# Attention behind a mixture of experts on one core: combines ahead of the normalising, two rooms for the first nine scores, two fills beside the last routed tiles

## The reference, cut to what matters

```
xn = _layernorm(x, axis=-1)
x = x + attn(xn) + ffn(xn)
...
scores = einsum('bshd,bthd->bhst', q, k) / sqrt(16)   # masked above the diagonal
out = softmax(scores) @ v ; out @ Wo + bo
...
routed = sum over a token's six experts of weight * (silu(g) * u) @ w_down
```

## Time and profile before

| what | us |
|---|---|
| median of 3 runs | 731.99 |
| lowest and highest | 728.43, 732.77 |
| the profiled execution: its time | 725.61 |
| its span, first to last instruction | 723.8 |
| PE busy in the span | 674.7 |
| DVE busy | 497.2 |
| POOL busy | 396.6 |
| ACT busy | 326.6 |

### The profile page before, as it was taken

One profiled execution on the slowest core, in us unless ns is written; L12 is line 12 of the kernel. 1 busy time (PEld: TensorE's weight loads), 2 busy tenths in 40 slices (PEclk: granted clock), 3 DMA queues, 4 the chain that ended last, 5 costly groups with the idle time before them and its releaser, 6 DMA issues.

```text
span 723.8 us, 19510 instructions
## 1 busy us (share of the span) xinstructions
PE 674.7 (93%) x5200; PEld 434.2 (60%) x5202; DVE 497.2 (69%) x1184; ACT 326.6 (45%) x849; POOL 396.6 (55%) x383
## 2 busy tenths in 40 slices
PE   6899999989999999999999999999778998999996
PEld 3755677664555555555555555555456776677764
DVE  5498899856666666667666666656377779777751
ACT  2432322224444444444444444444446566656552
POOL 2000000227787777777787776763776776677520
PEclk9599999999999999999999999999989999999998
DMA  8500000037676766767676763342122312231310
GB/s 282 185 1 1 1 0 1 22 112 233 191 211 195 224 211 214 224 211 214 211 224 191 248 210 98 98 96 58 59 66 73 100 55 67 88 98 57 96 59 30
DMA packets 54288, 90.75 MB, mean 125 GB/s; under 512 B 8694, under 2 KB 32438, under 8 KB 54246
## 3 DMA queue, kind: packets, MB, share of 16 engines
q1 hardware_dynamic: 23494, 43.11, 19.9%
q0 software_dynamic: 10752, 29.37, 14.4%
q10 hardware_dynamic: 20000, 17.73, 7.3%
HBM read 69.21 MB, written 20.97 MB: 125 GB/s over the span
## 4 chain that ended last, share of the span: by engine, by line
PE 61%; DVE 9%; POOL 8%; DMA 7%; issue 6%; ACT 3%; DVEq 2%; SPq 2%; ACTq 1%; POOLq 0%
PE pair L1023 20%; PE pair L1058 10%; PE pair L933 6%; POOL wqkv_sb L436 5%; DMA lower<-wdn 5%; PE pair L1009 4%; PE bank L1032 3%; PE pair L1042 3%; PE bank L996 3%; DMA wqkv_sb<-y_rows,slot_i 3%; PE bank L1134 2%; DVE negm L829 2%; DVE space L806 2%; POOL space L432 2%; PE bank L1081 1%
## 5 line engine op out<-in xcount | busy, mean ns | idle before, releaser
L380 POOL DMA_INDIRECT lower<-xn_rows,idx_all x128 | 136.9, 1069 | 228.4 <-DVE idx_all L752 135.5
L1023 PE MATMUL pair<-space,work 128*64 (+1 forms) x768 | 166.0, 463 | 7.9 <-DMA lower<-wdn 3.3
L1058 PE MATMUL pair<-lower,work 88*64 x512 | 121.6, 379 | 1.3 <-ACT work L537 1.0
L1023 PEld LDWEIGHTS pair<-space,work 128*64 128x64 f32 x768 | 66.9, 136 | 80.3 <-issue 56.5
L522 ACT ACTIVATE work<-pair 128x176 f32<-128x176 f32 x160 | 51.5, 322 | 117.4 <-PE pair L1023 59.9
L1058 PEld LDWEIGHTS pair<-lower,work 88*64 88x64 f32 x512 | 69.6, 137 | 48.1 <-issue 11.2
L762 DVE TENSOR_TENSOR work<-work,pair 128x176 f32<-128x176 f32 x160 | 53.1, 333 | 60.5 <-ACT work L522 60.0
L812 DVE COPY space<-lower 88x512 f32 x64 | 78.8, 1231 | 22.2 <-issue 21.8
L1023 PE MATMUL pair<-wqkv_sb,work 128*64 128x352 f32 x256 | 89.4, 472 | 0.0
L529 ACT ACTIVATE lower<-pair 128x256 f32<-128x256 f32 x128 | 49.3, 385 | 77.7 <-PE pair L1058 77.7
L557 ACT ACTIVATE pT<-pair 128x768 f32<-128x768 f32 x64 | 52.0, 812 | 58.9 <-PE pair L1121 56.2
(11 more groups left out here) (171 smaller groups left out, 1346.9 us busy)
## 6 DMA issues: line engine op xcount, KB each, us to landing
space<-wgu SPq DMA_DIRECT2D x66, 352.0 KB
y_rows<-lower ACTq DMA_DIRECT2D x128, 128.0 KB
lower<-wdn SPq DMA_DIRECT2D x66, 176.0 KB
x_all<-x SPq DMA_DIRECT2D x4, 512.0 KB, 7.7
xn_rows<-qk_all SPq DMA_DIRECT2D x16, 128.0 KB, 2.0
lower<-xn_rows,idx_all POOLq DMA_INDIRECT x128
out<-x_all SPq DMA_DIRECT2D x8, 256.0 KB, 2.5
wqkv_sb<-wqkv SPq DMA_DIRECT2D x1, 768.0 KB, 12.5
```

The source lines that it names most:

```text
L380: po.indirect_dma_start(xg[:, r % XB, :], None, xn_rows[:, :], bass.IndirectOffsetOnAxis(idx_all[:, r:r + 1], 0)).then_inc(xg_in[r % XB], 16)
L1023: last = pe.matmul(pair[u % 2][strip, 0:2 * F], xgT[u][:, c, strip], n, start=c == 0, stop=c == EC - 1, skip_group_check=True)
L1058: last = pe.matmul(pair[u % 2][strip, 512:512 + E], hT[:, u % 2, c, strip], n, start=c == 0, stop=c == 1, skip_group_check=True)
```

## The change

Four edits. In `d_slot` the combines of a slot stand directly behind its maxes, ahead of `normalise`, `halves` and `residual`. The scores of m < 9 go to `pair[m % 2]`, and their masks wait for all maxes up to m-2; `turned_masks(0)`, the first other user of `pair[1]`, waits for eight maxes. `fill(0)` and `fill(1)` are issued inside `down` of the last two routed tiles, ahead of its wait for the hidden rows, with waits of their own. The wait for `roped` moves with them.

```
+        def scores_at(m):
+
+            return pair[m % 2 if m < AHEAD else 0][:]
...
             def d_slot(n):
                 if 0 <= n + AHEAD < NS:
                     maxes(n + AHEAD)
+                if 0 <= n + SOONER < NS:
+                    for i in range((n + SOONER) * TOPK * NT // NS, (n + SOONER + 1) * TOPK * NT // NS):
+                        combine(i)
                 if n % 2 == 0 and 0 <= n // 2 - 2 < QUADS:
                     normalise(n // 2 - 2)
                 if n % 8 == 6 and 0 <= (n + 2) // 8 < B:
                     halves((n + 2) // 8)
                 if n % 8 == 5 and 0 <= (n - 13) // 8 < B:
                     residual((n - 13) // 8)
-                if 0 <= n + SOONER < NS:
-                    for i in range((n + SOONER) * TOPK * NT // NS, (n + SOONER + 1) * TOPK * NT // NS):
-                        combine(i)
...
+            def fill(f):
+
+                b, x = f // PAIRS_OF_HEADS, f % PAIRS_OF_HEADS
+                if x == 0:
+                    pe.wait_ge(padded, SB * (b + 1))
+                if f >= 2:
+                    pe.wait_ge(ring_ok, f - 1)
+                else:
+                    pe.wait_ge(xgT_ok, RT)
+                if f == 0:
+                    pe.wait_ge(roped, ROPES * NT)
...
             def down(i, u):
                 e = expert_of(u)
+                if isinstance(i, int) and TILES - 2 <= i:
+                    fill(i - TILES + 2)
                 pe.wait_ge(hT_ok, i + 1)
...
             def score_masks(m):
                 if m:
-                    pe.wait_ge(max_ok, m)
+                    pe.wait_ge(max_ok, m if m >= AHEAD else m - 1)
...
             def turned_masks(n):
                 if n:
                     pe.wait_ge(exp_done, n)
+                else:
+                    pe.wait_ge(max_ok, AHEAD - 1)
...
-                if 0 <= n + FILL < NS:
+                if 2 <= n + FILL < NS:
                     fill(n + FILL)
...
             pe.wait_ge(y_ok, RT)
-            pe.wait_ge(roped, ROPES * NT)
             pe.wait_ge(pad_ok, 1)
```

More of the change, by code:

```diff
@@ L823, in maxes @@
             def maxes(m):
-                scores = pair[0][:].rearrange("p (j k) -> p j k", j=2)
+                scores = scores_at(m).rearrange("p (j k) -> p j k", j=2)
                 dve.wait_ge(s_ok, m + 1)
@@ L1044, in down_shared @@
                 last.then_inc(dn_ok, 1)
+            def fill(f):
[8 more added lines that the diff above has]
+                    pe.wait_ge(roped, ROPES * NT)
+                for a in range(2):
+                    for s in range(SB):
+                        last = pe.transpose(bank[f % 2][:, (a * SB + s) * P:(a * SB + s + 1) * P],
+                                            qkp[:, b % 2, s, a, 2 * x:2 * x + 2].rearrange("p h i d -> p (h i d)"), id_f[:])
+                last.then_inc(tq_ok, 1)
             def down(i, u):
                 e = expert_of(u)
+                if isinstance(i, int) and TILES - 2 <= i:
+                    fill(i - TILES + 2)
                 pe.wait_ge(hT_ok, i + 1)
@@ L1070, in _ @@
             own = [slice(64 * j, 64 * (j + 1)) for j in range(2)]
[L1072 to L1083, removed]
             def score_masks(m):
                 if m:
-                    pe.wait_ge(max_ok, m)
+                    pe.wait_ge(max_ok, m if m >= AHEAD else m - 1)
                 for j in range(2):
-                    o = pair[0][:, 512 * j:512 * (j + 1)].rearrange("p (s k) -> p s k", s=2)[:, :, 0:P]
+                    o = scores_at(m)[:, 512 * j:512 * (j + 1)].rearrange("p (s k) -> p s k", s=2)[:, :, 0:P]
                     pe.matmul(o, id_b[:], mask_b[:].unsqueeze(1).to_broadcast([P, 2, P]), start=True, stop=False,
@@ L1097, in scores @@
                     for j in range(2):
-                        last = pe.matmul(pair[0][:, 512 * j + qt * P:512 * j + (2 * qt + 1) * P],
+                        last = pe.matmul(scores_at(m)[:, 512 * j + qt * P:512 * j + (2 * qt + 1) * P],
                                          q[own[j], qt * P:(qt + 1) * P], k[own[j], 0:(qt + 1) * P],
```

## The result

| | median us | lowest to highest | runs |
|---|---|---|---|
| before, same chip | 732.34 | 728.43 to 734.20 | 6 |
| after | 740.89 | 737.37 to 743.86 | 6 |

The ratio is 1.0125, with a 95% interval of 1.0079 to 1.0170: 9.2 us slower, between 5.8 and 12.4. The profiled execution after took 743.04 us with a span of 741.2, and the mean granted clock is 0.956 where it was 0.981.

The account below looks back on a forecast made before the run. Bound taken: PE at 61% of the span, and in the attention a ring of 24.14 us a batch. 0.4 + 0.05 + 4.15 + 2.2 = 6.8 us on the median 731.99 gave 738.8; range 735.5 to 741.5 (0.60).

Parts of the forecast that it names:

- the ring: Attention: chain from ACT's split through POOL's gathers to DVE's waiting slot 4 combine and the next split; 24.14 us a batch.
- the start: Up to slot 0: fills +0.5, two rooms -0.9, longer low clock +0.8; +0.4 us, bounds -0.9 and +1.8.
- C+0.98: Slot 5: earliest start of PE's projection, 0.98 us after the start C of the waiting slot 4 combine.
- The size of a batch without a fall: Slot 7's maxes and ACT's split 0.83 us later in each of five batches with a projection; 4.15, bounds 2 to 6.2.
- The 0.40 "won back": Slot 6: its combine, 0.40 us, is done during DVE's wait of 0.68 for `back`.
- The clock: PE idle 1.9 to 2.2 us ahead of projections: two of five fall, 1.1 each, 2.2 us; bounds 0 and 8.
- The first batch: Slot 4 without a projection: 0.45 us lost, 0.40 won back in slot 6, 0.05 in sum.
- The fills: Last two `down`s: `fill(0)` free, `fill(1)` delays the last `down`; 0.5 us, between 0 and 0.7.
- rival (b): Clock falls in nearly every batch and in slot 0: 12.5 us slower, 744.5; chance 0.15.
- Rival (d): Start not bound by the gather, two rooms' saving reaches slot 0, batches no longer: 728.5; chance 0.05.
- (c): Projection does not hold PE up, gathers landing earlier or `normalise` finding its place; only the start left: 731.8; chance 0.12.
- Rival (e): Combines delay POOL's subtraction in each batch, 0.48 x 5 on top of the forecast: 741.2; chance 0.08.

Follow-up runs that it names:

- the order alone: Kernel before with the combines of every slot moved ahead of normalise, halves and residual, nothing else; 742.26 us, +9.2 against before.
- slot 4 as before: Changed kernel with normalise ahead of the combines again in the slots 4 modulo 8 only; 727.42 us, -6.2 against before.
- work in the wait: Changed kernel with seven unread matmuls on PE ahead of the projection's wait for normalise; 736.67 us, +5.0 against before.
- the second profile of before: Kernel before, no edit, profiled once more on another chip; 732.17 us (one run).
- the rooms alone: Kernel before with only the first nine scores put in two rooms, fills and combines unmoved; 729.82 us, -2.5 against before.

## Why the prediction was right, and where it was off

The forecast was 738.8, and the median 740.89; on the run's own base, +6.8 against +9.2. The mechanism that carried it is shown: the ring, the projection in slot 5 behind a `normalise` behind the gather, and the falls of the clock. That the number came so near is in part luck: the order costs more than I had, and the start, which I had as a loss, is a gain.

**The projection behind the gather.** C+0.98 was forecast, and it is 0.98, 0.98, 0.99, 0.99 and 0.98. Undoing this one slot removes it.

**The size of a batch without a fall** was mis-sized: 0.83 forecast, 1.35 measured (25.36 against 24.01 for the same batch of before), 1.0 by the order alone (25.31 against 24.29). The forecast's distances of 24.9 to 26 were seen in one batch of the changed kernel; three were 27.0. (My mean of 24.14 runs from the second wait to the sixth, not the fifth; its value stands.) Three pieces make up the 0.52: the batch that I worked out was an unlucky one. Its two casts L841 took 0.42 and in others 0.24, so slot 7's maxes were at C+6.04 in it and at C+5.85 in the batch of 644.75; that is 0.19. The projection held PE 0.10 longer than I had (1.83 us from its start to that of the masks, 658.13 to 659.96, against 1.73); from there to `back` slot 6 took what it took before. And slot 0 took 0.19 more from its maxes to ACT's split (5.06 from 664.12 to 669.18, against 4.87). The 0.40 "won back" by the combine in slot 6 is largely given back there. With slot 4 as before, only that gain should be left, and the ring was 24.02 against 24.01 to 24.07:

```profile
654.41 1.03 DVE negm L833 x2
...
656.58 0.39 PE pair L1131 x4
...
659.48 0.52 ACT space L586
```

Slot 7's maxes start 5.64 after the combine in place of 5.85, but L1131, the products with the transposed maxima, takes 0.39 of the chain where it was 0.25, and the split comes 10.71 after the combine as it did before. That the missing piece is ACT's copy of those maxima, behind its split of slot 6, is argued from the order and not shown.

**The clock.** I counted two falls of 1.1; there were four, and a fall costs 1.6 (27.0 against 25.4; with the order alone there were three). PE's waits were 1.99, 1.93, 1.96, 1.87 and 1.93 us, at or just under the lower end of the 1.9 to 2.2 forecast. This term was 2.2 and measured 6.4 in this execution; with work in the wait it is gone. My way of judging it, by where 2.2 lies between a wait of 1.53 without a fall and one of 2.64 with one, had little under it. With the order alone 2.03 and 1.91 did not fall and 1.88, 1.97 and 1.94 did. And the fall of the earlier trace rows began at 525.5, 0.7 us into the wait of 2.64 (PE's last matmul ahead of it ended at 524.76), while the second profile of before fell at 516.6 behind waits of 1.22 and 0.61.

**The first batch**: 0.05 forecast. With work in the wait the distance behind it was 24.69, in the changed kernel 24.52, against 24.10 before; with the order alone it was 26.09 against 25.63. So 0.4 to 0.6; that this too is what was not won back in slot 6 is argued.

**The start** had the wrong sign: +0.4 forecast, -3.3 (-5.1 to -1.5) measured by itself. "The wait grows by what was saved, and this part brings nothing" held: the wait was 6.29 with the rooms alone, and combine 0 stood 16.9 us behind POOL's split in every profile. In the changed kernel the wait was 3.18 and not the 5 or more that I had announced; the clock was at 0.50 from 516.2 to 523.2 in it, and the early maxes came up to 2.20 apart. The step that failed is the base against which the start was reckoned. I took the low stretch of before to be the 7 us of the first profile, and charged +0.8 for the change making it longer. A typical execution of before has 24 us of it already, 20.5 in the slots around combine 0 and 3.4 behind combine 12, and with the rooms the way from combine 0 to 24 is 46.5 us in place of 49.6. I had seen that this execution was 6.4 under the median and put it aside with "the terms belong to waits between engines that each execution has". The clock stretches were not. The fills, +0.5 forecast, measured +1.9 (0.3 to 3.6).

**The sum.** The order measured 9.2 alone (I had 6.4), the start -3.3 alone; together they should be 5.9, which is just inside the interval of the change, 9.2 (5.8 to 12.4). So the two are neither shown to add up nor shown not to. The errors in the forecast went both ways and partly cancelled: the start was 3.7 us better than forecast, and if the parts add, the time without that would have been 744.6, rival (b)'s number. The profile of the changed kernel is in fact closer to (b), the clock falling in nearly every batch and in slot 0, than to the forecast: it has four falls of five, and the clock is at 0.50 through slots 0 and 1, up to 543.6. Rival (d) had a gain by the rooms, which came, but combine 0 still waited for its gather, and the ring did become longer. (c) was not seen: all five projections stood behind the gather. Rival (e) comes nearest in number, 741.2, and was not the cause: in every batch between 550 and 690 us POOL's first subtraction started ahead of the combines (670.39, the two combines at 670.89 took 2.49), and POOL's two subtractions take 1.28 and 1.42 of the chain where they took 1.28 and 1.43. The Trainium skill, "SBUF — State Buffer" (Who interferes with whom), would have the later one blocked, and here that was DVE, whose two combines take 1.00 elsewhere (530.57); this agrees.

## What to carry to other kernels

Before an instruction is moved ahead of another on an in-order engine, look for the one that will now stand behind a transfer, and ask who on other engines waits for it; one slot in eight made all of the loss, and keeping that slot, or moving the waiting combine by one slot (`SOONER` 3), turned 9 us of loss into 6 or 11 us of gain (with the start's part in both). One profile is one execution: take a second where the first lies at the edge of the timed runs, and look at the clock in both before a term is reckoned from either. The closing point of a ring is worth moving too: one slot later gave 5.3 us by itself, in a diff of one line, and made the new order worth another 6.

## What the runs showed of the hardware

- PE without a matmul for 1.93 to 1.99 us ahead of the projection was followed, within 1.1 us of the projection's start, by a granted clock of 0.50 for 3.4 us in four batches of the changed kernel; 1.87 us in the fifth left it at 1.00. With the order alone 1.88, 1.94 and 1.97 us were followed by a fall and 1.91 and 2.03 were not. So among waits of this length the length does not tell which one falls. In the kernel before, 1.53 us did no harm.
- The same early slots of the kernel before ran at 1.00 in one profile up to 525.5 and at 0.50 for 20 us in the other (516.6 to 537.1), and the clock stayed low there although PE was busy for 19.46 of the 20.00 us from 517 to 537.
- With seven matmuls that nobody reads in each wait, which left PE 0.39 to 0.49 us without work, no fall came behind a projection. Twelve of them ahead of slot 0 at SOONER 3 kept the clock at 1.00 there, and it fell at 542.1.
- Two combines took 1.00 us alone and 2.49 to 2.82 beside POOL's subtractions, whose first kept its 1.28 (changed kernel, 530.57, 670.89 and 585.75).
